# Attention scores of eight heads: rounded-fp32 parts, two heads in the array's 64-row halves

## What is computed

```
qkv = einsum('oc,bct->bot', qkv_w, h) + qkv_b[:, None]         # h: x normalised
q, k, v = each [8 images * 8 heads, 16, 1024]
w = softmax(einsum('bct,bcs->bts', q * scale, k * scale))       # 1024 x 1024 for each head
a = einsum('bts,bcs->bct', w, v)
out = x + einsum('oc,bct->bot', proj_w, a) + proj_b[:, None]
```

## Time and profile before

| | us |
|---|---|
| time, median of 3 runs | 2327.98 |
| lowest and highest run | 2327.2, 2330.86 |
| span of the profiled execution | 2324.5 |
| TensorE busy | 2210.8 (95%) |
| VectorE busy | 1817.7 (78%) |
| ScalarE busy | 1720.3 (74%) |
| GpSimd busy | 520.4 (22%) |

### The profile page before, as it was taken

The page is one execution under the profiler, slowest core; times in us unless marked ns, Lnnn a source line. Parts: engine busy times, 40 slices in busy tenths (PEclk is TensorE's granted clock), DMA queues, the critical chain, the costliest instruction groups (busy, mean ns, idle before and its releaser), DMA issues. The chain is left out here.

```text
span 2324.5 us, 34217 instructions
## 1 busy us (share of the span) xinstructions
PE 2210.8 (95%) x11776; PEld 974.3 (42%) x11776; DVE 1817.7 (78%) x3176; ACT 1720.3 (74%) x3107; POOL 520.4 (22%) x689
## 2 busy tenths in 40 slices
PE   3999999999999999999999999999998999999998
PEld 1223232323332232333233232323325888888887
DVE  2878878878887887888788878888846777777776
ACT  1467777767866776777777777777777888888887
POOL 3113030302213030212113030212003333333331
PEclk9999999999999999999999999999998999999999
DMA  8053361606243361616154251606102121121111
GB/s 153 10 66 58 52 79 44 94 20 91 44 65 60 51 89 25 100 26 88 34 77 62 47 79 33 105 22 91 25 16 75 43 67 57 42 66 57 42 52 48
DMA packets 81935, 136.86 MB, mean 59 GB/s; under 512 B 17760, under 2 KB 50656, under 8 KB 81632
## 3 DMA queue, kind: packets, MB, share of 16 engines
q1 hardware_dynamic: 78496, 133.90, 32.4%
q10 hardware_dynamic: 3264, 0.79, 0.2%
HBM read 57.31 MB, written 22.02 MB: 34 GB/s over the span
## 5 line engine op out<-in xcount | busy, mean ns | idle before, releaser
L450 DVE TENSOR_REDUCE h_half_nmax<-h_s_ps 128x1 f32<-128x512 f32 x2048 | 1286.8, 685 | 299.3 <-PE h_s_ps L689 292.3
L603 ACT ACTIVATE h_probs<-h_st_ps 128x512 f32<-128x512 f32 x2048 | 1104.2, 599 | 417.3 <-PE h_st_ps L826 411.4
L826 PE MATMUL h_st_ps<-h_qrep,h_krep 99*128 99x512 bf16 x2048 | 784.0, 384 | 54.1 <-issue 24.9
L689 PE MATMUL h_s_ps<-h_krep,h_qrep 96*128 96x512 bf16 x2048 | 799.6, 391 | 22.4 <-SPq L232 20.9
L681 PE MATMUL h_pv<-h_probs,h_vT 128*32 128x512 f32 x4096 | 552.0, 611 | 0.9 <-ACT h_probs L603 0.7
L689 PEld LDWEIGHTS h_s_ps<-h_krep,h_qrep 96*128 96x128 bf16 x2048 | 200.5, 98 | 682.4 <-DVE h_half_nmax L450 500.7
L826 PEld LDWEIGHTS h_st_ps<-h_qrep,h_krep 99*128 99x128 bf16 x2048 | 202.6, 99 | 251.5 <-issue 56.2
L1343 PE MATMUL o_s<-o_k,o_q 128*128 128x512 f32 x768 | 225.1, 429 | 7.4 <-DVE o_q L1164 5.7
L348 POOL TENSOR_SCALAR h_nparts<-h_nmax 128x16 bf16<-128x16 f32 x64 | 16.4, 256 | 956.0 <-DVE h_nmax L458 956.0
L1343 PE MATMUL o_pv<-o_pT,o_vT 128*128 128x512 f32 x768 | 207.3, 406 | 0.8 <-ACTq L1270 0.8
L1158 DVE TENSOR_TENSOR o_pT<-o_t,o_pT 128x512 fp32r<-128x512 f32 x256 | 164.6, 685 | 45.6 <-ACT o_pT L1295 43.1
(11 more groups left out here) (116 smaller groups left out, 1381.3 us busy)
## 6 DMA issues: line engine op xcount, KB each, us to landing
h_krep<-h_kp SPq DMA_DIRECT2D x96, 256.0 KB, 8.6
h_qrep<-h_qp SPq DMA_DIRECT2D x192, 128.0 KB, 9.5
x_res<-out_dram SPq DMA_DIRECT2D x32, 512.0 KB, 3.4
num<-av SPq DMA_DIRECT2D x128, 64.0 KB
rrep<-rden_dram SPq DMA_DIRECT2D x16, 512.0 KB
out_dram<-o_y SPq DMA_DIRECT2D x16, 512.0 KB
h_x_in<-out_dram SPq DMA_DIRECT2D x15, 512.0 KB, 3.4
out_dram<-h_y SPq DMA_DIRECT2D x15, 512.0 KB, 2.7
```

The source lines that it names most:

```text
L450: reduce = nc.vector.tensor_reduce(half_nmax[:, c, unit:unit + 1], s_ps[bank(2 * n + c)][:, :], AX.X, ALU.max, negate=True)
L603: nc.scalar.activation(probs[g % 2][:, j, :], st_ps[bank(n)][:, :], ACT.Exp, scale=1.0 / CH ** 0.5).then_inc(exp_done, 1)
L689: nc.tensor.matmul(s_ps[bank(n)][:, :], qrep[par][0:KS, th, head, tile * P:(tile + 1) * P], krep[par][0:KS, head, c * HALF:(c + 1) * HALF] ...
L826: nc.tensor.matmul(st_ps[bank(n)][:, :], krep[par][0:KM, head, st * P:(st + 1) * P], qrep[par][0:KM, th, head, :], start=True, stop=True). ...
```

## The change

q and k are now split into two parts in rounded fp32 (the type fp32r): ScalarE writes the rounded value, and one subtraction on GpSimd gives the rest. Three pairs of parts make 48 contraction rows, 51 with the maxima. Two heads are then held in partitions 0 to 50 and 64 to 114, and the matmuls of the two (r = 0 and 1) stand next to one another, each in its own 64 rows of the array and into its own bank. The weights of q and k are permuted to suit. TensorE's order within a group becomes: column scores of one pair of heads, row scores of a pair, products with values, column scores of the other pair, row scores, shared bank. The maxima's rows take two transfers where there was one, and `replicate` still has 18 of 256 or 128 KB. The ones are set at the very start.

```diff
-TERMS = 6
+TERMS = 3
+ROWS = P // 2
 KS = TERMS * CH
-KM = KS + 3
+MAX_PARTS = 3
+KM = KS + MAX_PARTS
...
-        qrep = [sb(f"qrep{i}", [P, 2, HEADS, HALF], BF16) for i in range(2)]
-        krep = [sb(f"krep{i}", [P, HEADS, T], BF16) for i in range(2)]
+        qrep = [sb(f"qrep{i}", [P, 2, HEADS // 2, HALF], F32R) for i in range(2)]
+        krep = [sb(f"krep{i}", [P, HEADS // 2, T], F32R) for i in range(2)]
...
-            tt, whole, (lead, middle, last) = engine.tensor_tensor, full[which][:, :], (parts[which][:, p, :] for p in range(3))
-            own.mark(tt(middle, whole, lead, ALU.subtract))
-            own.done(tt(rest[:, :], whole, lead, ALU.subtract))
-            own.done(tt(last, rest[:, :], middle, ALU.subtract))
+            own.done(engine.tensor_tensor(parts[which][:, 1, :], full[which][:, :], parts[which][:, 0, :].bitcast(F32),
+                                          ALU.subtract))
...
-                for term, part in enumerate((0, 1, 2, 0, 1, 0)):
-                    sp.dma_start(krep[par][term * CH:(term + 1) * CH, :, :], parts["k"][:, part, :]).then_inc(rep_dma, 16)
+                for term, part in enumerate((0, 0, 1)):
+                    for r in range(2):
+                        to, of = r * ROWS + term * CH, slice(r * ROWS, (r + 1) * ROWS)
+                        sp.dma_start(krep[par][to:to + CH, :, :].bitcast(F32),
+                                     parts["k"][of, part, :].bitcast(F32)).then_inc(rep_dma, 16)
...
+            for par in range(2):
+                for r in range(2):
+                    own.done(nc.gpsimd.memset(krep[par][r * ROWS + 32:(r + 1) * ROWS, :, :].bitcast(F32), 1.0))
+            pool.sem_inc(ones, 1)
...
-                own.done(nc.gpsimd.memset(krep[par][KS:KM, :, :], 1.0))
...
-                act.dma_start(qrep[par][KS:KM, th, quad * QUAD:(quad + 1) * QUAD, :],
-                              mrow[th][:, :]).then_inc(mrow_dma, 16)
+                for r in range(2):
+                    act.dma_start(qrep[par][r * ROWS + KS:r * ROWS + KM, th, quad * 2:(quad + 1) * 2, :].bitcast(F32),
+                                  mrow[th][r * MAX_PARTS * MP:(r + 1) * MAX_PARTS * MP, :].bitcast(F32)).then_inc(mrow_dma, 16)
...
+                    def column_scores(k, m):
+                        th, st = k // TILES, k % TILES
+                        for r in range(2):
+                            n = QUAD * (GROUPS * s + k) + 2 * m + r
+                            rows = slice(r * ROWS, r * ROWS + KM)
+                            pe.wait_ge(exp_done, last_in_bank(n) + 1 + QUAD)
+                            nc.tensor.matmul(st_ps[bank(n)][:, :], krep[par][rows, quad * 2 + m, st * P:(st + 1) * P],
+                                             qrep[par][rows, th, quad * 2 + m, :],
+                                             start=True, stop=True).then_inc(st_ready, 1)
...
+                        column_scores(k, 0)
+                        scores_ahead(k, 0)
+                        if not (first and s == 0 and k == 0):
+                            products(k - 1)
+                        column_scores(k, 1)
+                        scores_ahead(k, 1)
+                        in_shared_bank(k)
```

More of the change, by code:

```diff
@@ L105, in many_heads @@
     MH = UNITS // 2
+    MP = MH // 2
     LEAD = 12
@@ L152, in many_heads @@
         nrest = sb("nrest", [P, MH])
[L153 to L154 removed]
+        nparts = [sb(f"nparts{i}", [P, 2, MAX_PARTS, MP], BF16) for i in range(2)]
+        mrow = [sb(f"mrow{i}", [MAX_PARTS * MH, P], F32R) for i in range(2)]
         bst = sb("bst", [P, 2, 6])
@@ L444, in output, with maximum @@
                 dve.sem_inc(y_ready, 1)
-            def maximum(n, unit, offset=0):
-                for c in range(2):
-                    dve.wait_ge(scores_ready, 2 * (n + offset) + c + 1)
-                    reduce = nc.vector.tensor_reduce(half_nmax[:, c, unit:unit + 1], s_ps[bank(2 * n + c)][:, :],
+            def maximum(n, pair, c, offset=0):
+                th = pair // MP
+                for r in range(2):
+                    column = th * MH + r * MP + pair % MP
+                    dve.wait_ge(scores_ready, n + r + offset + 1)
+                    reduce = nc.vector.tensor_reduce(half_nmax[:, c, column:column + 1], s_ps[bank(n + r)][:, :],
                                                      AX.X, ALU.max, negate=True)
-                    if unit % MH != MH - 1 or c == 0:
+                    if pair % MP != MP - 1 or c == 0 or r == 0:
                         reduce.then_inc(max_done, 1)
@@ L476, in _ @@
             dve.sem_inc(misc_for_dve, -3)
-            for unit in range(2 * LEAD):
-                maximum(unit - 2 * LEAD, unit, 2 * LEAD)
+            for pair in range(LEAD):
+                for c in range(2):
+                    maximum(4 * (pair - LEAD) + 2 * c, pair, c, 4 * LEAD)
             dve.sem_inc(scores_ready, -4 * LEAD)
@@ L505, in body @@
                                 output(base + 4, 0, no_output)
-                        for unit in (2 * k, 2 * k + 1):
-                            if s % 2 == 1 and unit % 2 == 1 and STATS <= k < STATS + 4 and not (last and s == 3):
+                        for c in range(2):
+                            if s % 2 == 1 and c == 1 and STATS <= k < STATS + 4 and not (last and s == 3):
                                 if k == STATS:
@@ L510, in body @@
                                 statistics(k - STATS)
-                            if not (last and s == 3 and unit + 2 * LEAD >= UNITS):
-                                maximum(UNITS * s + unit, (unit + 2 * LEAD) % UNITS)
+                            if not (last and s == 3 and k + LEAD >= GROUPS):
+                                maximum(STEP * s + 4 * k + 2 * c, (k + LEAD) % GROUPS, c)
                     if s % 2 == 0:
@@ L811, in m_unit @@
                             return
-                        n = STEP * s + 2 * unit + half
-                        pe.wait_ge(max_done, last_in_bank(n) + 1 + 4)
-                        if m == 0 and half == 0 and ms % 2 == 0:
+                        if pair == 0 and c == 0 and ms % 2 == 0:
                             pe.wait_ge(rep_ready, u + 1)
-                        row_scores(n, ms // 2 % 2, ms % 2, m, half)
-                    for k in range(GROUPS):
-                        th, st = k // TILES, k % TILES
-                        if st == 0:
-                            pe.wait_ge(mrow_dma, 16 * (2 * s + th + 1))
-                        for j in range(QUAD):
-                            n = QUAD * (GROUPS * s + k) + j
-                            head = quad * QUAD + j
-                            pe.wait_ge(exp_done, last_in_bank(n) + 1 + QUAD)
-                            nc.tensor.matmul(st_ps[bank(n)][:, :], krep[par][0:KM, head, st * P:(st + 1) * P],
-                                             qrep[par][0:KM, th, head, :],
-                                             start=True, stop=True).then_inc(st_ready, 1)
-                            if j == 2 and not (first and n < QUAD):
-                                products(k - 1)
-                            m_unit(2 * k + j // 2, j % 2)
-                            if j == 3:
-                                in_shared_bank(k)
```

79 lines of the change are left out of this document (45 added, 34 removed).

## The result

| | before | after |
|---|---|---|
| median of the runs | 2327.59 us | 2626.47 us |
| lowest and highest run | 2326.67, 2330.86 | 2589.42, 2676.92 |
| ratio | | 1.1162, interval 1.1122 to 1.1202 |
| span of the profiled execution | 2324.5 us | 2645.9 us |

The changed kernel is slower by 11.6%. The prediction was 2317 us, with a range to 2370: wrong, and outside its range. Among the rivals, E (the low clock stays through odd steps) is the one that came, with a chance of 0.07 and put at "beyond 2400".

A forecast was written before the change was run, and what follows sets the result against it. TensorE was taken to bound the average, with transfers ending even steps. Even steps -38.4, clock +18, body edges +3, start +4.5 and last step +2.3 gave -10.6, hence 2317 us; range 2240 to 2370.

The forecast's parts named there:

- E: Rival, odd steps: TensorE waiting in every group keeps the low clock on; +166 if half are so, beyond 2400 us; chance 0.07.
- the term for the clock: Ends of even steps: TensorE's clock falls behind 9 of 16 waits of 2.3 us, 2.0 us each, +18 us.
- Plain groups: Groups without a projection: a loop over three `s_ps` banks sets 2.80 us, where 2.85 was read before.
- Groups with a projection: Groups with an fp32 projection product, partly hidden in the loop: 3.2 us, so -0.5; bounds 2.85 and 3.65.
- Odd steps: Plain groups, transposes, the second maxima DMA issue and statistics sum to about 0 change; bounds -1.6 and +1.3 us.
- Even steps: The transfer chain still ends them: -2.4 us each, to 52.3 us, -38.4 us over 16.
- The term of -1.4: Even steps' transfers of q and k: rows twice as long move faster, gaining 1.4 us; bounds 0 and -4.
- rival F: Even steps: longer rows gain nothing, -1.0 us each, -16 in place of -38.4; 2340 us, 2328 to 2350; chance 0.10.
- The -0.6 for projections ahead of the inversion: Even steps: two projections before VectorE's inversion, at -0.5 us each, of which 0.6 us was counted.
- D: Rival: the two halves don't run side by side; plain groups 2.93 us, total 2359 to 2367 us; chance 0.11.
- Start: Kernel start: memsets ahead of the first coefficients cost +8.3 us, less splits and transfer, giving +4.5 us.
- Last step: Last step: 12 groups without row scores go from 2.40 to 2.59 us with pairs, +2.3 us.

The follow-up runs named there:

- one_half: The changed kernel with all score matmuls on partitions 0 to 50, so that none can run beside another; 3858.47 us, ratio 1.6583.
- few_rows: The kernel before, with row scores on 32 contraction rows instead of 96 and column scores on 35 instead of 99; 4073.32 us, ratio 1.751.
- after_late: The changed kernel with six transfers of q's second half of queries held until the next step's maxima rows have landed; 2344.74 us, ratio 1.007.
- fill16: The changed kernel with two idle copies of each group's first column score, on 16 contraction rows instead of 51; 2478.21 us, ratio 1.0638.
- after_fill: The changed kernel with each group's first column score computed three times into the same bank (two useless copies); 2434.7 us, ratio 1.0478.
- prod_end: The changed kernel with the products with values moved from between the two pairs of column scores to the group's end; 2508.78 us, ratio 1.0758.
- smooth_same: The changed kernel reordered, each column score paired with a row score of the same half of the rows, transfers not held; 2642.83 us.
- smooth: The changed kernel reordered, each column score paired with a row score of the other half of the rows, transfers not held; 2371.22 us, ratio 1.0197.

## Why the prediction was wrong

- **The step that failed** is the term for the clock: "With waits of 2.3 us I expect it behind 9 of the 16, at 1.6 to 3 each, taken as 2.0: +18 (bounds 0 and +48)". The wait was right: 35.8 us in 15, 2.4 each. But the clock fell at 14 of them, and a fall costs not 2 us but up to 25 in the odd step (74.1 - 49.0) and some 6 more in the even step behind it (62.6 from 688.20 on, where others take 56), for the clock stayed low for up to 102.4 us. How long it stays differs from one wait to the next, and no run tells why. The price came from rows of before, and there it holds: the clock fell at two of its 15 waits, for 6.8 and 3.4 us. But in before every score fills 96 to 99 rows, one behind another. With 51 rows one_half never left the low pace and few_rows, with 32 to 35, neither. In pairs side by side the clock can return, but it often takes long. So the operation whose price was read in the old kernel was not the same in the new one. after_late shows the term's true size: 250 to 280 us hang on these waits.
- **Rival E** had the outcome (the low clock stays through odd steps), with too low a chance. Its reason was waiting in every group. In the slow odd steps TensorE hardly waits (73.78 of 74.10 us busy), nor does it in one_half and few_rows, so the low clock stays without such waits. That they can help to bring it about is not excluded: in the last step TensorE is busy for 8.41 us of the 10 from 2020 on, and then the clock falls.
- **Plain groups**: 2.80 predicted, 2.94 measured. The loop was the right one. Two of its terms were short: from the column pair to the row pair 0.34, not 0.23, and from a row score to its reduction 0.44, not 0.28; 1.00 + 0.34 + 0.44 + 0.74 + 0.43 = 2.95. Groups with a projection took 3.39 (products at 453.13 and 456.52), not 3.2. Odd steps at full clock take 49.0 in place of 46.8, outside the bounds given. The plain groups make under half of that; the rest stands in the groups with a transpose, a send or statistics (3.26 to 3.54 us, where before had 2.85 to 3.31), which were taken as a sum of about 0.
- **Even steps**: predicted 52.3, measured 55.8. From the inversion to TensorE's restart it is 38.2 us (459.49 to 497.70), where 36.9 was predicted and before had 38.65. Up to k's first transfer it gained the 0.4 that was counted. The longer rows gave nothing: from the first transfer of k to the restart it is 29.3 us in both (468.39 to 497.70, and 528.00 to 557.33). The term of -1.4 was 0, as rival F had it. By the Trainium skill, page "SBUF — State Buffer", section "Door 1: The DMA port swizzle (why `[64,N]` ≈ `[32,N]`)", what counts is how many of the 16 ports the touched partitions reach, and 16 neighbouring partitions reach four. The trace agrees in that nothing was gained: 115 to 126 GB/s with rows twice as long, 113 to 128 before; it doesn't show the ports. The -0.6 for projections ahead of the inversion did not come either (12.2 us from the step's first products to it, 12.0 before), and the restart now runs at the low clock, which takes 5.4 us to the step's end in place of 4.1. Also, only 15 of the 16 even steps have such transfers behind them.
- **D** did not come: the halves do run side by side. What TensorE saves by that at full clock shortens nothing, since the loop over the banks is longer.
- **Start** +6.1 (predicted +4.5). **Last step** +16.6 (predicted +2.3): the clock falls there too. Its groups take 2.67 us at full clock, where 2.59 was predicted.

What stays open: which measure of filling the chip uses, and how it weighs against waiting. fill16 against after_fill, one_half and few_rows show that the rows in use matter; the falls in prod_end and in last steps come at a full clock, with TensorE waiting a little in every group.

## What to carry to other kernels

Cutting contraction rows took nothing from the duration of a matmul here (0.43 us apart at the low clock with 51 rows as with 99) and can halve TensorE's clock; before packing or trimming rows, ask what fills the array in the new kernel, and don't price a fall of the clock by what it cost in the old one. A wait of 2 us cost little with scores on 99 rows and up to a whole stage at half speed with scores on 51, so remove the wait first, by sending only what is needed by then (six transfers held: 29 us in the old kernel, 250 to 280 in the new). Then shorten the loop over the banks: with the hold, pairs that fill one bank of either kind and products in two parts turned a loss of 11.6% into a gain of 3.7%.

## What the runs showed of the hardware

- TensorE at over 99% busy with 48- and 51-row scores in one half (one_half) kept the pace of 1.2 GHz for all of `many_heads` (0.43 us for 512 columns); with 32 to 35 rows in bf16 (few_rows) likewise. The same count of matmuls on 96 to 99 rows ran at 2.4 GHz in before (0.22 us).
- In smooth_same a matmul overtook the one written ahead of it, whose half of the rows was in use (both column scores at 207.83, the row score between them at 208.18).
- Matmuls of 35 rows stood 0.54 us apart at the low pace (few_rows), where those of 99 rows stood 0.43 apart (before, 500.83 to 501.26); their weight load wasn't hidden.
- The clock fell at 14 waits of 1.7 us or more in the changed kernel and at 14 in smooth, for 3.4 to 102.4 us in the one and 3.4 to 27.3 in the other, and in prod_end with no wait above 0.5 us ahead of it.
